# Six pairs of gathered rows on chip instead of four in two graph-attention walks, one hand-over of each kind per pair, and the next gather's index copy ahead of the window copy

## The reference

```python
N, E, HEADS, HID = 6250, 100000, 2, 128          # dst is sorted, src is random
def gat_layer(x, W, a_l, a_r, b, src, dst, num_nodes):
    z = (x @ W).reshape(num_nodes, heads, d)
    el, er = einsum('nhd,hd->nh', z, a_l), einsum('nhd,hd->nh', z, a_r)
    e = el[src] + er[dst];  e = where(e > 0, e, 0.2 * e)
    m = segment_max(e, dst);  ex = exp(e - m[dst]);  s = segment_sum(ex, dst)
    return segment_sum(z[src] * (ex / s[dst])[:, :, None], dst) + b
x = x + gat_layer(relu(gat_layer(layernorm(x), W1, ..)), W2, ..)     # two heads, then one
x = x + moe_ffn(layernorm(x))                                        # 8 experts, 2 per row
x = x + gnn(layernorm(x))      # segment_sum(x[src] * w, dst) / segment_sum(w, dst), two dense layers
x = x + routed_ffn(layernorm(x))
```

## Time and profile before

| what | value |
|---|---|
| median of 3 runs | 5531.81 us (5520.69 to 5536.3) |
| the profiled execution | 5476.3 us, its span 5474.4 us |
| granted TensorE clock over the span | 0.743 |
| busy share of the span | PE 57%, PEld 38%, DVE 36%, ACT 27%, POOL 49% |
| gathers of walk1, first to last issue | 213.9 to 1533.5 us |
| gathers of walk2 | 1635.5 to 2871.8 us |
| gathers of walk3 | 3728.7 to 4964.9 us |

### The profile page before, as it was taken

The page is one execution under the profiler, slowest core; times in us unless marked ns, Lnnn a source line. Parts: engine busy times, 40 slices in busy tenths (PEclk is TensorE's granted clock), DMA queues, the critical chain, the costliest instruction groups (busy, mean ns, idle before and its releaser), DMA issues. The chain is left out here.

```text
span 5474.4 us, 64894 instructions
## 1 busy us (share of the span) xinstructions
PE 3105.6 (57%) x13336; PEld 2063.1 (38%) x13336; DVE 1945.2 (36%) x5614; ACT 1503.9 (27%) x4807; POOL 2672.5 (49%) x2732
## 2 busy tenths in 40 slices
PE   4155555556652545455454489921555565656699
PEld 3144444444431222222223478810333333333466
DVE  4254455545432333233336822151222222222322
ACT  2122222222221222222221023311344344344223
POOL 1355556555516666666662145525656556551121
PEclk9567777777676777777775699965777777777799
DMA  6356566556623333333334256684444444442111
GB/s 152 82 91 106 96 101 102 97 105 102 98 54 96 93 94 93 94 91 95 92 94 124 73 192 221 220 233 127 113 114 117 113 114 116 114 112 71 54 56 57
DMA packets 381424, 598.27 MB, mean 109 GB/s; under 512 B 102442, under 2 KB 272078, under 8 KB 380658
## 3 DMA queue, kind: packets, MB, share of 16 engines
q0 software_dynamic: 136000, 386.29, 31.6%
q1 hardware_dynamic: 209138, 172.22, 11.7%
q10 hardware_dynamic: 36160, 38.56, 2.3%
HBM read 489.46 MB, written 107.34 MB: 109 GB/s over the span
## 5 line engine op out<-in xcount | busy, mean ns | idle before, releaser
L727 PE MATMUL walk_ps_part<-walk_rows,walk_whot 128*80 128x129 f32 (+1 forms) x4704 | 1109.6, 382 | 78.6 <-issue 78.5
L583 POOL DMA_INDIRECT walk_rows<-z_two_heads,walk_idx x784 | 779.2, 994 | 606.8 <-ACT walk_idx L597 375.1
L583 POOL DMA_INDIRECT walk_rows<-z_one_head,walk_idx x784 | 769.1, 981 | 569.2 <-ACT walk_idx L597 317.1
L1856 POOL DMA_INDIRECT walk_rows<-h,walk_idx x784 | 743.0, 948 | 523.9 <-ACT walk_idx L1870 270.1
L727 PEld LDWEIGHTS walk_ps_part<-walk_rows,walk_whot 128*80 128x80 f32 x4704 | 727.7, 186 | 343.1 <-issue 280.3
L2002 PE MATMUL walk_ps_part<-walk_rows,walk_whot 128*80 128x257 f32 x1568 | 498.2, 453 | 126.4 <-issue 84.2
L629 ACT ACTIVATE walk_window<-walk_ps_part 80x258 f32<-80x258 f32 (+1 forms) x196 | 74.8, 382 | 1225.8 <-remote 914.4
L620 ACT ACTIVATE walk_whot<-walk_hot,walk_w 128x80 f32<-128x80 f32 x1568 | 405.7, 346 | 20.8 <-ACT walk_w L611 15.0
L2002 PEld LDWEIGHTS walk_ps_part<-walk_rows,walk_whot 128*80 128x80 f32 x1568 | 250.3, 174 | 299.5 <-issue 249.5
L696 PE MATMUL walk_ps_row_scores<-keep_ident,walk_fmax 32*1 32x32 f32 (+1 forms) x98 | 18.4, 188 | 598.2 <-issue 312.9
L725 PE MATMUL walk_ps_part<-walk_window,walk_carry 80*1 80x129 f32 (+1 forms) x588 | 166.9, 372 | 158.4 <-issue 79.7
(11 more groups left out here) (365 smaller groups left out, 4661.4 us busy)
## 6 DMA issues: line engine op xcount, KB each, us to landing
exp_w<-in_ffn_W SPq DMA_DIRECT2D x108, 512.0 KB
agg<-walk_window ACTq DMA_DIRECT2D x198, 80.3 KB
walk_rows<-z_two_heads,walk_idx POOLq DMA_INDIRECT x784
walk_rows<-z_one_head,walk_idx POOLq DMA_INDIRECT x784
comb_ya<-y_tokens POOLq DMA_DIRECT2D x28, 448.0 KB
walk_rows<-h,walk_idx POOLq DMA_INDIRECT x784
walk_erB<-er_two_heads SPq DMA_DIRECT2D x104, 80.0 KB
agg<-walk_window ACTq DMA_DIRECT2D x99, 80.6 KB
```

What stands on the lines that cost most here:

```text
L583: pool.indirect_dma_start(out=Z[k // 2][:, k % 2 * GROUP_TILES + t, :], out_offset=None, in_=table, in_offset=bass.IndirectOffsetOnAxis(ap ...
L727: last = pe.matmul(P[k % 2][0:WIN, cols], S[k % HOTS][:, h, t, :], Z[k // 2][:, k % 2 * GROUP_TILES + t, h * HS:h * HS + HW], start=t == 0 ...
L1856: pool.indirect_dma_start(out=Z[k // 2][:, k % 2 * GROUP_TILES + t, :], out_offset=None, in_=table, in_offset=bass.IndirectOffsetOnAxis(ap ...
```

## The change

It touches three things.

1. In `edge_walk` UNROLL becomes 12 (EDGE_UNROLL): 6 pair buffers `Z`, 12 index buffers, 6 sets of inputs, and loops of 6 pairs instead of 4. The group `s` now takes the place of `s - 12`. SyncE loads 5 pairs ahead instead of 3, and the node numbers are made 8 steps ahead instead of 6. The 98 groups are 8 turns of 12 and 2 more, as they were 12 turns of 8 and 2 more. The first phase computes two more loop counts.
2. The chain of maxima is spread over more pairs. TensorE turns `el` four pairs ahead of the products, at the end of a pair. `turn_ends` of the pair `p + 3` and `turn_ins` of the pair `p + 2` become one stage, `turn_rows`, between the two steps of a pair, and `columns` of the pair `p + 1` comes first in the pair. VectorE's `scan_rows` does `carries` of one pair and `scan_maxima` of the pair before it, and `scan_el` stands last. So `el_turned`, `rows_turned` and `cols` are given once per pair, where `el_turned`, `ends_turned`, `ins_turned` and `cols` were. `el` is turned into a PSUM bank of its own and copied once per pair to SBUF (`el_rows`), two small copies and a drain are added, and `firsts` keeps a pair's first values.
3. In all three walks `window` reads its two table entries before its wait, and copies the next gather's indices (`copy_idx`) right behind the wait for `done8`, ahead of the window copy and its store.

```diff
+EDGE_UNROLL = 12
+EDGE_LOOPS = (GROUPS - 2) // EDGE_UNROLL
+LONG_PAIRS = -(-(MAX_STEPS - 2) // (UNROLL * EDGE_UNROLL // 4)) * (UNROLL * EDGE_UNROLL // 8)
+LONG_LOOPS, EDGE_LONG = 2 * LONG_PAIRS // UNROLL, 2 * LONG_PAIRS // EDGE_UNROLL
+STEP_TAB = 2 * 104
+assert EDGE_LOOPS * EDGE_UNROLL + 2 == GROUPS and 2 * LONG_PAIRS + 2 + EDGE_UNROLL <= STEP_TAB
...
+    UNROLL = EDGE_UNROLL
...
-        LOCAL_AHEAD = 6
+        LOCAL_AHEAD = 8
...
+        ends = ph.sb("ends", [1, CT1, H])
+        firsts = [ph.sb(f"firsts{k}", [1, 2, H]) for k in range(2)]
+        el_rows = [ph.sb(f"el_rows{k}", [ROWS, TILE]) for k in range(2)]
...
+        psT = ph.ps("el", [128, 512])[0:ROWS, 0:TILE]
         rows_bank = ph.ps("row_scores", [128, 512])
-        psT = rows_bank[0:ROWS, 0:TILE]
-        psR = rows_bank[0:1, TILE:TILE + 2 * ROWS]
-        psK = rows_bank[0:ROWS, TILE + 2 * ROWS:TILE + 2 * ROWS + 2]
+        psR = rows_bank[0:1, 0:2 * ROWS]
+        psK = rows_bank[0:ROWS, 2 * ROWS:2 * ROWS + 2]
...
-        AHEAD = 3
+        AHEAD = 5
...
             def window(s, k, started):
-                n0 = first_node(act, s)
+                n0, after = first_node(act, s), group(act, s + UNROLL)
                 act.wait_ge(done8, s + (UNROLL + 1))
+                copy_idx(after, k)
                 if started is not None:
                     act.wait_ge(stored, started)
                 act.activation(wsb[k % 2][:, :], P[k % 2][0:WIN, 0:AW], ACT.Copy).then_inc(win_ready2, 1)
                 act.wait_ge(win_ready2, s + 3)
                 act.dma_start(agg[bass.ds(n0, WIN), 0:AW], wsb[k % 2][:, :]).then_inc(stored, 16)
-                copy_idx(s + UNROLL, k)
                 local(s + LOCAL_AHEAD, (k + LOCAL_AHEAD) % UNROLL)
...
+            def turn_rows(r, ends_too, ins_too):
+
+                if ends_too:
+                    pe.wait_ge(el_scanned, r + 1)
+                    pe.sem_inc(row_tick, 1)
+                if ins_too:
+                    pe.wait_ge(rows_ready, r)
+                    pe.sem_inc(row_tick, 1)
+                    pe.matmul(psK[:, 0:1], ends[:, 0:PT, :].rearrange("o t h -> o (t h)"), ones[:, 0:1], start=True, stop=True)
+                    last = pe.matmul(psK[:, 1:2], begins[:, 1:CT1, :].rearrange("o t h -> o (t h)"), ones[:, 0:1],
+                                     start=True, stop=True)
+                if ends_too:
+                    pe.transpose(psR[:, 0:ROWS], Fl[:, TILE - 1:TILE], ident[0:ROWS, 0:ROWS])
+                    last = pe.transpose(psR[:, ROWS:2 * ROWS], Bl[:, 0:1], ident[0:ROWS, 0:ROWS])
+                last.then_inc(rows_turned, 1)
+
+            def columns(p, k):
...
+            def pair(p, m, s, turn, on):
+
+                if on(1):
+                    columns(p + 1, (m + 1) % 2)
                 products(s, 2 * m, 0)
-                if turn is not None:
-                    turn_el(p + 2, b, turn)
                 products(s, 2 * m, 1)
                 if node:
                     node.turn(pe, p, m % 2)
                 products(s, 2 * m, 2)
-                if turn is not None:
-                    turn_ends(p + 2)
                 products(s, 2 * m, 3)
                 if node:
                     node.products(pe, p, m % 2)
-                products(s + 1, 2 * m + 1, 0)
-                if turn is not None:
-                    turn_ins(p + 2)
-                for quarter in range(1, 4):
+                if on(2):
+                    turn_rows(p + 3, on(3), True)
+                for quarter in range(4):
                     products(s + 1, 2 * m + 1, quarter)
-                if turn is not None:
-                    columns(p + 2)
+                if on(4):
+                    turn_el(p + 4, (m + 4) % PAIRS, turn)
...
-                turn_ends(p)
-                turn_ins(p)
-                columns(p)
+                turn_rows(p, True, p > 0)
+            turn_el(2, 2, 1)
+            columns(0, 0)
+            turn_rows(2, True, True)
+            turn_el(3, 3, 1)
...
+            def scan_el(p, q, k, loaded):
+                dve.wait_ge(inputs[q], loaded)
                 dve.wait_ge(el_turned, p + 1)
                 dve.tensor_tensor_scan(Fl[:, :], R[q][:, 0:TILE], psT[:, :], -BIG, ALU.add, ALU.max)
                 dve.tensor_tensor_scan(Bl[:, TILE - 1::-1], R[q][:, TILE:0:-1], psT[:, TILE - 1::-1], -BIG,
                                        ALU.add, ALU.max)
-                dve.tensor_copy(ends[:, 0, :], ends[:, PT, :])
-                dve.drain().then_inc(ends_ready, 1)
-
-            def carries(p, q):
-                dve.wait_ge(ends_turned, p + 1)
-                turned = psR[:, :].rearrange("o (c t h) -> o c h t", c=2, h=H)
-                reset = rr[q][:, :, :, :, :].rearrange("o c h j t -> o c h (j t)")
-                for h in range(H):
-                    dve.tensor_tensor_scan(ends[:, 1:CT1, h], reset[:, 0, h, :], turned[:, 0, h, :],
-                                           ends[:, 0, h:h + 1], ALU.add, ALU.max)
-                    dve.tensor_tensor_scan(begins[:, PT - 1::-1, h], reset[:, 1, h, ::-1], turned[:, 1, h, ::-1],
-                                           -BIG, ALU.add, ALU.max)
-                dve.drain().then_inc(ins_ready, 1)
-                dve.tensor_tensor(foremost, ends[:, 0, :], begins[:, 0, :], ALU.max)
-
-            def scan_maxima(p, q):
-                dve.wait_ge(ins_turned, p + 1)
-                dve.tensor_copy(gkc[:, :], psK[:, :])
-                dve.drain()
-                dve.tensor_tensor_scan(Cf, R[q][:, 0:TILE], psT[:, :], gkc[:, 0:1], ALU.add, ALU.max)
-                dve.drain()
-                dve.tensor_tensor_scan(M[:, TILE - 1::-1], R[q][:, TILE:0:-1], Cf[:, TILE - 1::-1], gkc[:, 1:2],
-                                       ALU.add, ALU.max)
-                dve.drain().then_inc(max_ready, 1)
+                dve.tensor_copy(el_rows[k][:, :], psT[:, :])
+                dve.drain().then_inc(el_scanned, 1)
+
+            def scan_rows(r, q, k, ends_too, ins_too):
+
+                dve.wait_ge(rows_turned, r + 1)
+                if ins_too:
+                    dve.tensor_copy(gkc[:, :], psK[:, :])
+                if ends_too:
+                    turned = psR[:, :].rearrange("o (c t h) -> o c h t", c=2, h=H)
+                    reset = rr[q][:, :, :, :, :].rearrange("o c h j t -> o c h (j t)")
+                    dve.tensor_copy(ends[:, 0, :], ends[:, PT, :])
+                    dve.drain()
+                    for h in range(H):
+                        dve.tensor_tensor_scan(ends[:, 1:CT1, h], reset[:, 0, h, :], turned[:, 0, h, :],
+                                               ends[:, 0, h:h + 1], ALU.add, ALU.max)
+                        dve.tensor_tensor_scan(begins[:, PT - 1::-1, h], reset[:, 1, h, ::-1], turned[:, 1, h, ::-1],
+                                               -BIG, ALU.add, ALU.max)
+                    dve.drain()
+                    dve.tensor_tensor(firsts[k][:, 0, :], ends[:, 0, :], begins[:, 0, :], ALU.max)
+                    dve.tensor_copy(firsts[k][:, 1, :], ends[:, 0, :])
+                dve.drain().then_inc(rows_ready, 1)
+                if ins_too:
+                    before = (q + INS - 1) % INS
+                    dve.tensor_tensor_scan(Cf, R[before][:, 0:TILE], el_rows[1 - k][:, :], gkc[:, 0:1], ALU.add, ALU.max)
+                    dve.drain()
+                    dve.tensor_tensor_scan(M[:, TILE - 1::-1], R[before][:, TILE:0:-1], Cf[:, TILE - 1::-1], gkc[:, 1:2],
+                                           ALU.add, ALU.max)
+                    dve.drain().then_inc(max_ready, 1)
...
+            def scores(m, s):
+
                 hot(s, 2 * m % UNROLL)
                 hot(s + 1, (2 * m + 1) % UNROLL)
-                carries(p, q)
-                targets(q, 0, 2 * m % UNROLL)
-                scan_maxima(p, q)
-                targets(q, 1, (2 * m + 1) % UNROLL)
+                dve.drain()
+                for j in range(2):
+                    targets(m % INS, j, (2 * m + j) % UNROLL)
...
+            def pair(p, m, s, half, loaded, on):
 
                 weights(p + 1, m + 1, s + 2)
-                if turn is not None:
-                    scores(p + 2, m + 2, s + 4, turn)
+                if on(2):
+                    scores(m + 2, s + 4)
                 if node:
                     node.scale(dve, p + 1, (m + 1) % 2, half)
+                if on(2):
+                    scan_rows(p + 3, (m + 3) % INS, (m + 3) % 2, on(3), True)
+                if on(4):
+                    scan_el(p + 4, (m + 4) % INS, m % 2, loaded)
```

93 lines of the change are left out of this document (39 added, 54 removed).

## The result

The changed kernel takes 5375.56 us (median of 4 runs, 5360.57 to 5401.25), the kernel before 5526.65 us beside it (4 runs, 5520.69 to 5536.3): ratio 0.973, 95% interval 0.9686 to 0.9774. So it is faster, by 151 us; the forecast was 5220 us, about twice the gain. The profiled execution took 5360.57 us (span 5358.9 us).

The account below looks back on a forecast made before the run. It took GpSimd's stalls between runs of gathers, with TensorE's signals seen late, as the bound. Savings of 159 us (walk1), 82 (walk2) and 66 (walk3), together 307, gave 5169 us, scaled to 5220 us; range 4980 to 5430 us.

Parts of the forecast that it names:

- What bounds the kernel: In the walks, no engine fills a pair; GpSimd stalls because TensorE's signals are seen late while gathers are issued.
- The index copy first: In `window`, reads before the wait and copy right behind it save 1.6 us per stall; 66 us in walk3.
- The ring fills again and a stall comes again: In walks 1 and 2, despite six pairs on chip, stalls return and cost 3.8 us each.
- Three groups for each stall: In walks 1 and 2, 1.5 pairs pass per stall: 2.5 us of stall and 23.2 us per pair.
- This round trip (L629 to L725): In every step `products` needs TensorE to ScalarE and back, which the change keeps, so the ring fills again.
- the second rival: One stall per pair stays in walks 1 and 2, only the copy's place gains: 24.5 us a pair, 5349 us; chance 0.25.
- the sign of that rival: GpSimd's runs in walks 1 and 2 would be of 16 gathers, where the forecast had 24 or so.
- The tails: Behind the last gather TensorE works off two pairs more: 24 us lost in walk1, 17 us in walk2.
- At the start nothing is lost: Before the first gathers the change costs nothing, since GpSimd's first groups need no free buffer.
- merely earlier: SyncE's loads keep their size, come earlier and wait for the same logits as before; no cost was put on them.
- The first rival: Gathers never pause in the walks, GpSimd alone bounds them: 20.7 us a pair, 553 us off, 4973 us; chance 0.17.

Follow-up runs that it names:

- the pair of traces from one chip: Kernel before and changed kernel, each run once more unaltered on one further chip: 5466.94 us (one run) and 5324.33 us (ratio 0.9722).
- the changed kernel with the table reads: Changed kernel plus three reads of a table entry into a GpSimd register behind each group of gathers in walks 1 and 2: 4712.35 us (one run).
- that one group: Experiments adding GpSimd drains or table reads behind groups of gathers, on a chip where the kernel before took 4668.75 us: 5706.09, 5209.92, 5162.87 and 4712.35 us.

## Why the prediction was half right

**What bounds the kernel: right.** GpSimd's stalls behind runs of gathers, set by TensorE's signals: without gathers the signals come in 0.12 us and the walks shrink to 853 and 523 us; with almost no bytes in them nothing changes. What in the gathers holds them, issue or landing, is open.

**The index copy first: right, and all of the gain.** Priced at 1.6 us per stall. In walk3, where nothing else changed, each wait fell from 6.3 us (270.1 in 43) to 4.65 us (232.4 in 50), and the walk by 54 us for the 66 us forecast (70 us in the pair of traces from one chip). GpSimd starts 0.8 us behind the copy's end (2137.36 to 2138.16), as put. What I had not seen is that this edit is the whole change: copy alone 0.9705 and 0.9677, ring and chain without it 0.9995. (The edit moves the table reads and the copy together; which of the two gives how much was not tried.)

**The ring fills again and a stall comes again, 3.8 us each: right in walk2.** Measured 3.9 and 4.1 us there; walk1's are shorter, 2.7 us, and more.

**Three groups for each stall: this step failed.** I had argued that the chain a pair further ahead lets two or three steps through. Walk2 shows two, as before, and walk1 one. In walk2's timeline it is one released in the stall, one within some 2 us of its end; then `products` needs the window of the step before, whose release is TensorE's own late signal. The prediction named this round trip (L629 to L725) as the reason why the ring fills again, and then did not apply it to the number of steps per stall. Neither ring nor chain touches it. In walk2, with 16 gathers per stall, the second rival gives 24.5 us a pair and 24.1 us were measured. In walk1 the sign of that rival, runs of 16, did not come: 76 stalls in 49 pairs, 4.8 us of stall per pair in place of the forecast's 2.5 us, and 25.3 us a pair. Why walk1 lets only one group through was not tried. Together this is 146 us of the forecast lost in walks 1 and 2 (183 and 99 us forecast before tails, 80 and 56 us measured). The rest of the 192 us between the forecast's 307 and the measured 115.5 us: 12 us in walk3, 27 us in the two tails, 12 us at the start, less 5 us at the end. These parts are of two traces that may be of two chips; in the pair from one chip walk1 and walk2 fell by 69 us each (138 us for the same 282 us forecast), so the step that failed is the same.

**Walk1 by itself.** The chain (or the loads further ahead, which came with it) does shorten it, by some 50 us, but only with the copy first (1315.3 us with ring and chain alone, 1297.3 us with ring and copy, 1239.3 us with all). Why the two work only together was not tried.

**The tails: right in kind, too small.** Behind the last gather, TensorE's carry products of after and, from the earlier trace rows, of before. Walk2 and walk1 of after and walk1 of before, last rows:

```profile
2845.15 0.59 PE L739 MATMUL walk_ps_part<-walk_window,walk_carry 80*1 80x257 f32 x2
```

```profile
1561.88 0.38 PE L739 MATMUL walk_ps_part<-walk_window,walk_carry 80*1 80x129 f32 x2
```

```profile
1589.76 0.59 PE L725 MATMUL walk_ps_part<-walk_window,walk_carry 80*1 80x129 f32 x2
```

Walk2's last stands 54.9 us behind the last gather, before 32.9 us: 22 us for 17. Walk1's stands 96.4 us behind it, before 56.3 us (1589.76 less 1533.5): 40 us for 24, since its two pairs cost some 20 us each, near the 17.6 us that the walk without gathers needs, and not 12.

**"At the start nothing is lost": wrong, 12 us.** I looked for free buffers and not at SyncE's queue. It issues six pairs of loads ahead now, not four, and the constants of the second table stand behind them. The index copies of ScalarE wait for these constants; of after, and of the copy alone:

```profile
225.08 0.21 ACT L608 ACTIVATE walk_idx<-keep_src 128x8 int32 x1 [58.54 <-DMA walk_n_bcol<-in_b_gat]
```

```profile
209.00 0.21 ACT L596 ACTIVATE walk_idx<-keep_src 128x8 int32 x1 [46.84 <-DMA walk_n_bcol<-in_b_gat]
```

That is 16 us later, and in the run with the ring and the old AHEAD of 3 the first gather is at 205.0 us. From one chip the first gather of before is at 211.5 us and of after at 226.7 us. The prediction had called the loads "merely earlier", without the queue that they are put ahead of.

**The rivals.** One stall per pair (5349 us) comes nearest to what happened; it was given 0.25 against 0.46. Its mechanism held in walk2; in walk1 its figure came out near (25.3 us a pair for 24.5) by other means, which is luck. In sum the walks saved 191 us for its 222, and tails and start cost 75 us for its 41. The first rival, gathers that never pause, is what the chip without the lateness showed in the changed kernel with the table reads; of the kernel before there is only the time there, 4669 us, and no trace. The Trainium skill (TensorE: Matmul & The Clock Gate, The cost: per-tile semaphore tail) has a signal cost tens of nanoseconds; the trace of that chip does not contradict it (0.13 us from the products' end to the copy's start), those of the others do while gathers are issued.

**What stays open.** Why TensorE's signals are late on some chips and not on one. Outside that one group every profiled kernel with unbroken gathers showed the stalls, and all runs of the kernel before lie between 5450 and 5538 us; no chip served two of the five groups, so chip and moment are not told apart. The changed kernel itself was not run where signals are on time.
